# A graph network in one kernel: earlier z loads, statistics aggregated in two steps, and message-table zeroing moved into the second convolution's loop

## The chip, the cores and the metric

The kernel runs on one core of a Trainium2 chip (trn2). The metric is the device time of one execution in microseconds (us); the figure for the kernel before is the median of three. One execution was also taken by the hardware profiler, and all rows quoted here are of that one.

Engine names: PE is TensorE (PEld its weight loads), DVE is VectorE, ACT is ScalarE, POOL is GpSimd, SP is SyncE, which here only issues transfers. Each engine works through its own instructions in order and waits on semaphores.

## What is computed

6250 nodes with 128 features, 100000 edges sorted by destination. Two graph convolutions, then one edge-wise message layer whose batch normalisation needs the mean and variance over all edges:

```python
h = relu(layernorm(x))
x = x + conv2(relu(conv1(h)))        # conv: (segment_sum(h[src], dst) / max(deg, 1)) @ W_nbr + h @ W_root + b
h = relu(layernorm(x))
z = concatenate([h[src], h[dst], edge_attr], axis=1) @ W.T + b
mean, var = mean(z, axis=0), mean(square(z - mean(z)), axis=0)
z = (z - mean) * rsqrt(var + eps) * gamma + beta
msg = sigmoid(z[:, :128]) * softplus(z[:, 128:])
out = x + h + zeros.at[src].add(msg)
```

## The kernel before

**Tiles.** Nodes are padded to NT = 49 tiles of 128. Edges are padded to NG = 196 groups of 512, each GT = 4 tiles of 128. All stages run one after the other inside one launch.

**Second convolution** (about 950 to 1795 us of the profile). POOL gathers rows of h by source, PE sums them by destination with one-hot matrices. In the gaps between groups two side jobs run. One is the root product (one per node tile; x comes by `load_x`). The other is a sort: 98 jobs compute, for every edge, its place (`pos_i`) in a table `m_tab` ordered by source window. Each sort job needs one row of a base table, which SP loads with `load_base` (1.5 KB) into one buffer `brow`; PE waits for it (`srt.base_in`) before it adds it to the ranks (L1645, L1646), and after PE's `srt.ranked` SP loads the next.

**Zeroing.** `m_tab` has SG = 292 groups of 512 rows in DRAM: FIRST = 160 that are summed while messages are still made, then LAST = 132. It must be zero before messages are scattered, since places are not all filled. `zero_rows(g, n)` (L637) is one transfer on SP's queue that writes n groups of 264 KB. Of the 292 groups 160 are zeroed in the second convolution: 3 in each of the 48 turns of SP's loop at L668, right behind a `load_base`, and 16 at once in one transfer after the loop, ahead of the last `load_base` (job 97). The other 132 are zeroed in pass 2. `sg.rows_zeroed` counts the transfers; ACT and SP wait for the first 49 before the memory that holds the zeros is used for something else, and POOL before its first scatter.

**Pass 1** (1848 to 3058). For every group PE computes z (256 x 512 values) in PSUM; ACT copies it to SBUF (L1008), SP stores it to `z_tab` in DRAM (L703, `p1.z_stored`), and DVE's `count_z` takes batch statistics of it (L1400, two instructions a group), LATE = 3 groups behind its own one-hot step (L1393). `p1.stats_done` counts these.

**Between the passes.** After group 195 DVE aggregates all 196 statistics, once for each half of z (L1424), and works out scale and shift with ACT's square root between (L1426 to L1431, `norm.ready`). POOL clears the pads (`ms.pads_zeroed`, L814) and, once all z are stored and all statistics taken, the sums `MSUM` (L818, `sg.sums_zeroed`); DVE waits for that before its first step of pass 2. ACT and DVE set the semaphores `ms.abs_ready` and `ms.dve_step` to RZ = 8 when `norm.ready` has come, so that SP's waits for them hold its first z load back until then.

**Pass 2** (3073 to 4256, and the last sums to 4398). Turns of eight groups, d = 0, 1, ..., s = 0 to 7, in a ring of RZ = 8 buffers `zin`. SP loads z of a group (L736, 512 KB) and behind it zeroes rows: for d = 0, 3 or 2 groups each (20 in all), for d = 1 to 14 one each. ACT works in fours: sigmoid (L1024, `gates`), absolute value (L1027), exp (L1033), log (L1038), each as four instructions in a row, and between them it copies finished rows (L1045, L1046, `ms.row_ready`). DVE scales z (L1458), adds (L1465) and multiplies (L1473). PE turns the messages back (L1775). POOL scatters every tile of 128 rows into `m_tab` (L828, four a group). From group 112 on the first 160 groups of `m_tab` are read back (L716) and summed (PE L1766, DVE L1450 and L1443) beside pass 2, and the last 132 after the last scatter.

## Time and profile before

| | |
|---|---|
| median of 3 runs | 3799.49 us (3788.65 to 3800.49) |
| span of the profiled execution | 4398.3 us |
| mean clock granted to TensorE in it | 0.780 |
| PE busy | 2818.5 us (64%) |
| POOL busy | 2548.5 us (58%) |
| DVE busy | 1869.5 us (43%) |
| ACT busy | 1407.3 us (32%) |

The profiled execution took longer than the timed ones, by 598.8 us. So the rows give places and durations in one slower execution. The page cuts the span into 40 slices of 110 us: slices 9 to 16 are the second convolution, 17 to 27 pass 1, 28 to 38 pass 2, 39 and 40 the last sums. In a timeline row the first number is the start, the second the time from the first instruction of the row to the end of its last, the bracket the idle time of the engine before it and what ended it.

### The profile page before, as it was taken

To read this page: it belongs to the slowest core of one execution; us is meant where nothing else is said; L and a number is where in the kernel's file an instruction comes from. 1 tells how busy PE (TensorE), PEld (TensorE's weight loads), DVE (VectorE), ACT (ScalarE), POOL (GpSimd) and SP (SyncE) were. 2 spreads that over 40 slices of the span, in tenths; PEclk is the share of its full clock that TensorE was granted. 3 is DMA by queue.
4 is the path that set the end of the run, shared out by engine and by line. 5 is a ranking of instruction groups with operands and counts; after the bars stand their busy time and mean duration, and the time that the engine had idled before them with its cause. 6 is when DMAs were issued, how large, how long until landed. Compare 5 with 4: busy or idle time off the path is not lost.

```text
span 4398.3 us, 65055 instructions
## 1 busy us (share of the span) xinstructions
PE 2818.5 (64%) x14957; PEld 1886.6 (43%) x15051; DVE 1869.5 (43%) x4062; ACT 1407.3 (32%) x2631; POOL 2548.5 (58%) x2545
## 2 busy tenths in 40 slices
PE   1777777767778877677788788887112211466639
PEld 1455455544555545544444444443111111455538
DVE  6444444454444444732222223223323232456638
ACT  2222222221000000422222221222777677666730
POOL 4556455545564654166666666664577777776750
PEclk9778788867788888888888889888555555677759
DMA  3222222234433434267777677776755555677638
GB/s 102 83 82 69 72 71 83 89 86 133 148 126 117 150 127 161 89 202 242 245 238 242 232 237 244 236 230 206 256 171 195 186 185 182 207 239 239 228 120 271
DMA packets 339103, 750.12 MB, mean 171 GB/s; under 512 B 66424, under 2 KB 130268, under 8 KB 333856
## 3 DMA queue, kind: packets, MB, share of 16 engines
q1 hardware_dynamic: 242656, 497.83, 33.3%
q0 software_dynamic: 93440, 218.82, 16.8%
q10 hardware_dynamic: 2880, 32.11, 2.1%
q8 instruction: 38, 0.62, 0.1%
q14 instruction: 89, 0.73, 0.1%
HBM read 465.29 MB, written 283.22 MB: 170 GB/s over the span
## 4 chain that ended last, share of the span: by engine, by line
PE 47%; issue 18%; another core or an unknown queue 12%; ACT 11%; DVE 7%; DVEq 3%; DMA 1%; ACTq 0%; SPq 0%; POOL 0%; POOLq 0%
PE PS L1750 9%; PE PS L1745 8%; PE PS L1583 6%; PE PS L1573 6%; PE PS L1766 5%; PE PS L1736 5%; PE PS L1569 2%; ACT H L1024 2%; ACT arena L1033 1%; ACT arena L1027 1%; PE PS L1646 1%; ACT arena L1038 1%; ACT L1033 1%; ACT L1038 1%
## 5 line engine op out<-in xcount | busy, mean ns | idle before, releaser
L796 POOL DMA_INDIRECT Q<-h_tab,src_i x960 | 952.4, 992 | 723.2 <-issue 261.9
L828 POOL DMA_INDIRECT m_tab<-Q,pos_i x784 | 829.6, 1058 | 359.3 <-issue 230.0
L1775 PE MATMUL PS<-ident,arena 128*128 128x128 f32 x784 | 198.9, 403 | 712.4 <-issue 377.9
L1583 PE MATMUL PS<-Q 128*128 x2684 | 476.3, 331 | 234.9 <-DVE Q L1162 111.1
L796 POOL DMA_INDIRECT H<-p_tab,src_i x400 | 382.4, 956 | 338.5 <-DMA p_tab<-arena 112.4
L1583 PEld LDWEIGHTS PS<-Q 128*128 128x128 f32 x2684 | 408.3, 231 | 325.4 <-issue 321.7
L1008 ACT ACTIVATE arena<-PS,LB 128x512 f32<-128x512 f32 x392 | 242.1, 686 | 937.5 <-remote 699.1
L796 POOL DMA_INDIRECT arena<-p_tab,src_i x384 | 364.9, 950 | 209.9 <-issue 108.4
L1775 PEld LDWEIGHTS PS<-ident,arena 128*128 128x128 f32 x784 | 130.0, 202 | 775.0 <-issue 521.7
L1745 PE MATMUL PS<-H,Q 128*128 x1371 | 387.4, 418 | 88.8 <-issue 84.2
L1750 PE MATMUL PS<-arena,WC 128*128 128x512 f32 x784 | 415.1, 654 | 25.7 <-issue 25.7
L1400 DVE BATCH_NORM_STATS2 stats<-arena 128x512 f32 (+1 forms) x392 | 253.0, 684 | 252.9 <-ACT arena L1008 209.1
L1393 DVE TENSOR_SCALAR H<-arena,wpos 128x512 int16 x244 | 89.6, 367 | 584.2 <-issue 297.6
L1766 PE MATMUL PS<-Q 128*128 128x128 f32 x1872 | 266.7, 305 | 85.6 <-issue 76.8
L1766 PEld LDWEIGHTS PS<-Q 128*128 128x128 f32 x1872 | 255.0, 220 | 93.4 <-issue 80.0
L1162 DVE SCALAR_TENSOR_TENSOR Q<-dst_f,wneg,iota 128x512 f32 x322 | 242.0, 752 | 121.7 <-issue 120.8
L1745 PEld LDWEIGHTS PS<-H,Q 128*128 x1464 | 152.4, 105 | 261.5 <-issue 159.0
L1750 PEld LDWEIGHTS PS<-arena,WC 128*128 128x128 f32 x784 | 167.3, 215 | 178.3 <-issue 153.9
L1152 DVE TENSOR_TENSOR arena<-arena,PS x380 | 107.9, 284 | 319.1 <-PE PS L1587 159.1
L1569 PE MATMUL PS<-Q 128*128 128x392 bf16 x336 | 127.5, 393 | 153.9 <-issue 84.2
L1045 ACT COPY Q<-PS 128x512 f32<-128x512 f32 x196 | 112.6, 575 | 326.9 <-remote 266.4
L1450 DVE TENSOR_TENSOR Q<-Q,iota 128x512 f32<-128x512 f32 x234 | 160.5, 686 | 60.2 <-DMA Q<-m_tab 58.6
(232 smaller groups left out, 4434.4 us busy)
## 6 DMA issues: line engine op xcount, KB each, us to landing
z_tab<-arena SPq DMA_DIRECT2D x196, 512.0 KB
Q<-z_tab SPq DMA_DIRECT2D x196, 512.0 KB
Q<-m_tab SPq DMA_DIRECT2D x234, 264.0 KB
arena<-in_edge_t SPq DMA_DIRECT2D x196, 256.0 KB
m_tab<-arena SPq DMA_DIRECT2D x48, 792.0 KB
m_tab<-src_i SPq DMA_DIRECT2D x112, 264.0 KB
arena<-dst_tab SPq DMA_DIRECT2D x196, 128.0 KB
count_tab<-Q SPq DMA_DIRECT2D x11, 1568.0 KB
```

The source lines that it names most:

```text
L796: nc.gpsimd.indirect_dma_start(row(s, k), None, table, bass.IndirectOffsetOnAxis(src_i[:, t:t + 1], 0)).then_inc(landed[s], 16)
L828: nc.gpsimd.indirect_dma_start(m_tab, bass.IndirectOffsetOnAxis(pos_i[:, t:t + 1], 0), mrow[:, s, k, :], None).then_inc(ms.scattered[s], 16)
L1008: ins = nc.scalar.activation(zb[:, s, h * GE:(h + 1) * GE], PS[:, 2 * s + h, :], ACT.Identity, bias=LB[:, h:h + 1])
L1162: v.scalar_tensor_tensor(onehot[:, ds(n % k.banks, 1), 0:n_tiles * P].rearrange("p a (t b) -> p (a t) b", b=P), bc(dst, P), wneg[:, ds(w, 1)],
L1400: ins = v.bn_stats(stats[:, h, ds(g, 1), :].rearrange("p a b -> p (a b)"), zb[:, s, h * GE:h * GE + valid])
L1573: return mm(PS[:, 4, 0:cols], item_sums(par)[:, v, :], part_of(v, v + 1)[:, :, 0:cols].rearrange("p a b -> p (a b)"), start=v == 0, stop=v ...
L1583: ins = mm(pair_sums(m % k.banks, slice(0, F)), row(t), oh[:, t * P:(t + 1) * P], start=t == 0, stop=t == n_tiles - 1, skip_group_check=True)
L1736: mm(PS[:, 2 * s + h, k * P:(k + 1) * P], p_row(u, k)[:, h * F:(h + 1) * F], ident[:], is_transpose=True, start=k == 0, stop=False, skip_g ...
L1745: ins = mm(PS[:, 2 * s + h, :], part, hot, start=False, stop=False, skip_group_check=True)
L1750: ins = mm(PS[:, 2 * s + h, :], WC[:, h * F:(h + 1) * F], ebuf[:, s, :], start=False, stop=True, skip_group_check=True)
L1766: ins = mm(PS[:, SD + o % SD, 0:F], mrow_in[o % MR][:, t, 0:F], shot[:, o % SD, t * P:(t + 1) * P], start=t == 0, stop=t == GT - 1)
L1775: ins = turn(PS[:, 2 + q, t * P:(t + 1) * P], msg_t[:, q, t * P:(t + 1) * P], ident[:])
```

## The change

Four things:

1. SP's loop in the second convolution zeroes 4 groups in each of its first ZN = 45 turns (180 groups) and none in the last 3. The transfer of 16 groups is gone. The 20 groups of pass 2's d = 0 are gone; d = 1 to 14 is as before (112 groups). All waits count transfers anew (45, and 45 + 112).
2. The z loads of d = 0 wait no more for `ms.dve_step` and `ms.abs_ready`, only for what stands ahead of pass 2 on SP: PE done, all z stored. The wait for `ms.pads_zeroed` moves behind the eighth of them.
3. After its last one-hot step, and before `count_z` of groups 193 to 195, DVE aggregates the statistics of groups 0 to 192 (`fold_early`): two aggregations, and then for each half three small instructions that write the result as the record of group 192, with its count.
4. The aggregation after group 195 covers four records: that one and groups 193 to 195.

```diff
-    ZG, REST = 3, 16
-    ZFIRST = [3, 3, 3, 3, 2, 2, 2, 2]
+    ZG, ZN = 4, 45
+    BEFORE = ZG * ZN
+    EARLY = NG - LATE
...
-            with sp.Fori(0, NT - 1) as i:
-                sp.wait_ge(srt.ranked, i * 2 + 1)
-                load_base(i * 2 + 1)
-                sp.wait_ge(root.product, i + 1 + NT)
-                load_x(i + 1)
-                sp.wait_ge(srt.ranked, i * 2 + 2)
-                load_base(i * 2 + 2)
-                zero_rows(i * ZG, ZG)
-            zero_rows(FIRST - REST, REST)
+            for i0, i1 in ((0, ZN), (ZN, NT - 1)):
+                with sp.Fori(i0, i1) as i:
+                    sp.wait_ge(srt.ranked, i * 2 + 1)
+                    load_base(i * 2 + 1)
+                    sp.wait_ge(root.product, i + 1 + NT)
+                    load_x(i + 1)
+                    sp.wait_ge(srt.ranked, i * 2 + 2)
+                    load_base(i * 2 + 2)
+                    if i1 == ZN:
+                        zero_rows(i * ZG, ZG)
             sp.wait_ge(srt.ranked, JOBS - 1)
             load_base(JOBS - 1)
...
-                    sp.wait_ge(ms.dve_step, g + 1)
-                    sp.wait_ge(ms.abs_ready, g + 1)
+                    if not (isinstance(d, int) and d == 0):
+                        sp.wait_ge(ms.dve_step, g + 1)
+                        sp.wait_ge(ms.abs_ready, g + 1)
                     sp.dma_start(zin[:, s, :], square(z_tab, g)).then_inc(ms.z_in[s], 16)
-                if isinstance(d, int) and d == 0:
-                    zero_rows(FIRST + sum(ZFIRST[0:s]), ZFIRST[s], src_i[:].bitcast(F32)[:, 0:GT * MW])
-                elif not isinstance(d, (int, Mid)):
-                    zero_rows(d * RZ + (FIRST + sum(ZFIRST) - RZ + s), 1, src_i[:].bitcast(F32)[:, 0:GT * MW])
+                if not isinstance(d, (int, Mid)):
+                    zero_rows(d * RZ + (BEFORE - RZ + s), 1, src_i[:].bitcast(F32)[:, 0:GT * MW])
+                if isinstance(d, int) and (d, s) == (0, RZ - 1):
+                    sp.wait_ge(ms.pads_zeroed, 1)
...
-            sp.wait_ge(ms.pads_zeroed, 1)
             in_eights(sp, LAG, pass2)
...
-                    pool.wait_ge(sg.rows_zeroed, 16 * (NT + MID * RZ))
+                    pool.wait_ge(sg.rows_zeroed, 16 * (ZN + (MID - 1) * RZ))
...
+            def aggregate(h, g0, g1):
+                return v.bn_aggr(bn[:, 2 * h:2 * h + 2], stats[:, h, g0:g1, :].rearrange("p a b -> p (a b)"))
+
+            def fold_early():
+
+                dve.wait_ge(p1.stats_done, EARLY)
+                for h in range(2):
+                    step(aggregate(h, 0, EARLY))
+                for h in range(2):
+                    folded = stats[:, h, EARLY - 1, :].rearrange("p (k c) -> p k c", c=3)
+                    v.memset(folded[:, :, 0:1], EARLY * GE / 2.0)
+                    v.tensor_copy(folded[:, :, 1:2], rep(bn[:, 2 * h:2 * h + 1], 2))
+                    step(v.tensor_scalar(folded[:, :, 2:3], rep(bn[:, 2 * h + 1:2 * h + 2], 2), EARLY * GE / 2.0, None, ALU.mult))
+
             def pass1(i, s):
                 if back(i, s, 0):
                     onehot_by_window(i, s, pair)
+                if isinstance(i, int) and (i, s) == (ITER, 0):
+                    fold_early()
...
             for h in range(2):
-                step(v.bn_aggr(bn[:, 2 * h:2 * h + 2], stats[:, h].rearrange("p a b -> p (a b)")))
+                step(aggregate(h, EARLY - 1, NG))
```

What SP issues around the end of its loop in the second convolution, in the kernel before (L657 is `load_base`, L665 `load_x`, L637 `zero_rows`; its loop starts at L668):

```order
L657 ISA [waits sort_ranked]
L657 DMA Q<-base_tab 1x392
L637 ISA
L637 DMA m_tab<-arena 128x3x528
L668 REGISTER_ALU
L668 COMPARE_AND_BRANCH
L637 DMA m_tab<-arena 128x16x528
L657 DMA Q<-base_tab 1x392 [waits sort_ranked]
```

And in the changed kernel, where the same lines are L658 and L638 and the loop L670:

```order
L658 ISA [waits sort_ranked]
L658 DMA Q<-base_tab 1x392
L638 ISA
L638 DMA m_tab<-arena 128x4x528
L670 REGISTER_ALU
L670 COMPARE_AND_BRANCH
L670 UNCONDITIONAL_BRANCH
L670 ISA
```

The transfer of four groups takes the place of that of three, and a second loop without a zeroing follows where the transfer of 16 groups was.

SP at the start of pass 2, before:

```order
L736 DMA Q<-z_tab 128x1024 [waits pass1_done,msg_pads_zeroed,pass1_z_stored3,msg_dve_step,pass1_z_stored2,msg_abs_ready,pass1_z_stored1,pass1_z_stored0]
L637 DMA m_tab<-src_i 128x3x528
L736 DMA Q<-z_tab 128x1024 [waits msg_abs_ready,msg_dve_step]
L637 DMA m_tab<-src_i 128x3x528
L736 DMA Q<-z_tab 128x1024 [waits msg_abs_ready,msg_dve_step]
```

And now:

```order
L739 DMA Q<-z_tab 128x1024 [waits pass1_z_stored3,pass1_z_stored2,pass1_done,pass1_z_stored1,pass1_z_stored0]
L739 DMA Q<-z_tab 128x1024 x7
L450 UNCONDITIONAL_BRANCH [waits msg_pads_zeroed]
L450 ISA
L739 ISA [waits msg_abs_ready,msg_dve_step]
```

Eight z loads stand in a row, without the two waits and without zeroing between them.

DVE at the end of pass 1, before:

```order
L1400 BN_STATS stats<-arena 128x6 [waits pass1_z_ready]
L1400 BN_STATS stats<-arena 128x6
L1424 BN_AGGR bn<-stats 128x2 [waits pass1_stats_done]
L1424 BN_AGGR bn<-stats 128x2 [waits dve_chain]
L1426 TENSOR_SCALAR bn<-bn 128x2 [waits dve_chain]
```

And now (three pairs of statistics stand behind the early aggregation, of which the first is shown):

```order
L1412 BN_AGGR bn<-stats 128x2 [waits pass1_stats_done]
L1412 BN_AGGR bn<-stats 128x2 [waits dve_chain]
L1421 MEMSET stats 128x2 [waits dve_chain]
L1422 COPY stats<-bn 128x2
L1423 TENSOR_SCALAR stats<-bn 128x2
L1421 MEMSET stats 128x2 [waits dve_chain]
L1422 COPY stats<-bn 128x2
L1423 TENSOR_SCALAR stats<-bn 128x2
L1402 BN_STATS stats<-arena 128x6 [waits pass1_z_ready,dve_chain]
```

The long aggregation moved ahead of the last three pairs of statistics, and a short one stands behind them.

## Rows read from the trace of the kernel before

**Rows 1.** The page: span, granted clock and DMA share in 40 slices.
```profile
span 4398.3 us, 65055 instructions
PEclk9778788867788888888888889888555555677759
DMA  3222222234433434267777677776755555677638
```
**Rows 2.** Timeline: end of pass 1 and the steps between the passes.
```profile
3046.66 1.29 DVE L1400 BATCH_NORM_STATS2 stats<-arena 128x512 f32 x2 [0.28 <-ACT arena L1008]
...
3059.34 0.55 DVE L1400 BATCH_NORM_STATS2 stats<-arena 128x6 f32<-128x160 f32 x2 [2.52 <-ACT arena L1008]
3059.93 10.96 DVE L1424 BATCH_NORM_AGGREGATE bn<-stats 128x2 f32<-128x1176 f32 x2
3062.08 5.32 POOL L818 MEMSET arena<- 128x6272 f32 x1 [3.33 <-DMA z_tab<-arena]
...
3072.75 0.16 DVE L1431 TENSOR_TENSOR bn<-GB,bn 128x2 f32<-128x2 f32 x1
```
**Rows 3.** Timeline: start of pass 2 up to the first scatter.
```profile
3073.17 1.28 ACT L1024 ACT_TABLE_LOAD   x1 [1.83 <-DVEq L1491]
3073.23 0.35 SPq L736 DMA_DIRECT2D Q<-z_tab  x1
...
3077.54 0.81 ACT L1024 ACTIVATE H<-Q,bn 128x512 f32<-128x512 f32 x1 [3.09 <-DMA Q<-z_tab]
...
3080.87 0.81 ACT L1024 ACTIVATE H<-Q,bn 128x512 f32<-128x512 f32 x1 [2.52 <-DMA Q<-z_tab]
...
3087.54 0.81 ACT L1024 ACTIVATE H<-Q,bn 128x512 f32<-128x512 f32 x1 [2.51 <-DMA Q<-z_tab]
...
3096.65 0.69 DVE L1465 SCALAR_TENSOR_TENSOR arena<-H,arena 128x512 f32<-128x512 f32 x1 [5.21 <-ACT arena L1038]
...
3103.87 1.01 POOL L828 DMA_INDIRECT m_tab<-Q,pos_i  x1 [36.47 <-DMA m_tab<-src_i]
```
**Rows 4.** Stretches: bounds, length, busy us of PE PEld DVE ACT POOL, clock, DMA share, GB/s.
```profile
3067.00:3073.00 6.00, 0.00 (x0) 0.00 (x0) 5.36 (x10) 0.20 (x1) 0.40 (x1) 0.50 0.00 0
3078.00:3083.00 5.00, 0.00 (x0) 0.00 (x0) 0.63 (x2) 1.16 (x2) 0.00 (x0) 0.50 1.05 412
```
**Rows 5.** Pass 2's scatters: their group on the page; last one; waits from 3100 to 3900.
```profile
L828 POOL DMA_INDIRECT m_tab<-Q,pos_i x784 | 829.6, 1058 | 359.3 <-issue 230.0
...
4255.34 0.97 POOL L828 DMA_INDIRECT m_tab<-Q,pos_i  x1 [0.30 <-issue]
...
POOL m_tab L828 <- ACT Q L1046: 60.9, 22, 4.7
```
**Rows 6.** Timeline: last sort jobs of the second convolution; SP's transfers, and PE.
```profile
1737.89 0.33 PE L1645 MATMUL PS<-Q,upper_bf 128*128 128x392 bf16 x1
...
1739.00 2.05 PE L1583 MATMUL PS<-Q 128*128 x16
...
1739.79 1.06 SPq L637 DMA_DIRECT2D m_tab<-arena  x2
...
1743.87 2.44 SPq L657 DMA_DIRECT2D Q<-base_tab  x1
...
1754.80 0.48 PE L1645 MATMUL PS<-Q,upper_bf 128*128 128x392 bf16 x1 [7.16 <-issue]
...
1756.82 3.78 PE L1583 MATMUL PS<-Q 128*128 x16
```
**Rows 7.** The same columns as rows 4, around the transfer of 16 groups.
```profile
1742.00:1754.00 12.00, 5.64 (x34) 3.55 (x31) 4.13 (x9) 0.53 (x2) 0.00 (x0) 0.89 1.04 386
1754.00:1758.00 4.00, 3.20 (x8) 1.78 (x9) 1.04 (x2) 0.00 (x0) 0.00 (x0) 0.50 0.01 4
```
**Rows 8.** SP within the loop, and what PE's L1645 waited for in all (us, times).
```profile
1020.08 0.42 SPq L637 DMA_DIRECT2D m_tab<-arena  x1
1023.21 0.23 SPq L657 DMA_DIRECT2D Q<-base_tab  x1
...
  DMA Q<-base_tab: 53.8, 26
```

More of the change, by code:

```diff
@@ L88, in build_gnn @@
     assert JOBS == PAIRS * MID_SORTS + 2 * END_SORTS and NT == PAIRS * MID_ROOTS + 2 * END_ROOTS
-    ZG, REST = 3, 16
-    ZFIRST = [3, 3, 3, 3, 2, 2, 2, 2]
+    ZG, ZN = 4, 45
+    BEFORE = ZG * ZN
+    EARLY = NG - LATE
     assert FIRST % PER == 0 and PER % SD == 0 and MID * RZ >= SCAT + RZ and MID + MIDS < DITER
-    assert FIRST == (NT - 1) * ZG + REST and LAST == sum(ZFIRST) + (MID - 1) * RZ
+    assert SG == BEFORE + (MID - 1) * RZ and BEFORE >= FIRST and ZN < NT
     HALF = NG // 2
@@ L692, in _ @@
             sp.wait_ge(pq.product, CP + len(SUBS) * 3)
-            sp.wait_ge(sg.rows_zeroed, 16 * NT)
+            sp.wait_ge(sg.rows_zeroed, 16 * ZN)
             for s in range(SL):
@@ L819, in _ @@
             pool.wait_ge(srt.pos_ready, JOBS)
-            pool.wait_ge(sg.rows_zeroed, 16 * NT)
+            pool.wait_ge(sg.rows_zeroed, 16 * ZN)
             for g in range(NG):
@@ L970, in _ @@
                     squares(1)
-            act.wait_ge(sg.rows_zeroed, 16 * NT)
+            act.wait_ge(sg.rows_zeroed, 16 * ZN)
             def turned_h(i):
```

## Prediction

> **What bounds the kernel now.** I read the page first. The profiled execution spans 4398.3 us, and the slices show no single bound [rows 1]: in the second convolution no resource is full, in pass 1 the engines run with PE, and from slice 28 on PE's clock stands near half because PE has little to do. So the question at each edit is which wait ends last at its place. Then I read the timeline between the passes, stretches for the DMA share, the scatter rows, and the timeline of the second convolution's end.
>
> Between the passes one chain runs. The last statistics end at 3059.34 + 0.55 = 3059.89, the two aggregations take 10.96 us, and scale and shift are ready at 3072.75 + 0.16 = 3072.91 [rows 2]. Only then SP issues the first z load, at 3073.23; ACT's first gate starts at 3077.54, so 4.31 us from issue to use. The next gates follow at 3.33 us each (3077.54 to 3087.54 is three such steps), though a gate takes 0.81 us: each waits for its z [rows 3]. Why 3.33: between two z loads (524288 bytes) stands a zeroing of 811008 bytes, and the DMA share is 1.05 at 412 GB/s, which is full [rows 4]. 1335296 bytes in 3.33 us are 401 GB/s. From the end of gate four (3088.35) to the first scatter (3103.87) are 15.52 us of work on ACT, DVE and PE in series [rows 3].
>
> From there POOL's scatters are the bound: 784 of them at 1.058 us, and 0.30 us between two, make 1065 us. They run from 3103.87 to 4256.31, which is 1152 us; of the other 87 us, 61 are short waits for rows from ACT in the first 800 us [rows 5]. ACT in turn works behind the same ring. Whatever starts this chain earlier ends it earlier, since nothing in it is tied to a fixed time. The last 132 sums follow the last scatter.
>
> At the end of the second convolution PE stood idle for 7.16 us before the last sort job's L1645 [rows 6]. The row says "issue", but SP's queue tells why: the last two zeroings (3 and 16 groups, 5.14 MB) were issued from 1739.79, the base row of 1.5 KB for this job at 1743.87 behind them. The DMA share is 1.04 until 1754 and 0.01 after [rows 7], and PE starts at 1754.80. The base row waited behind the zeros.
>
> **Part 1, the transfer of 16 groups goes.** The base row of job 97 then has an idle queue. In the loop the next base row was in use about 2 us after issue; I take 2 (the mean of the 26 waits for such rows is 53.8 / 26 = 2.07 us [rows 8]), so it is there at 1745.9, before PE comes at 1754.80 - 7.16 = 1747.64. The 7.16 us go in full. More goes with them: after the pause PE runs at half clock, 16 matmuls in 3.78 us against 2.05 before it. From the start of L1645 to the end of these 16 it was 1760.60 - 1754.80 = 5.80 us, two jobs before it 1741.05 - 1737.89 = 3.16 [rows 6]. So 2.6 more, if PE keeps its clock. Sum 9.8 us; bounds 7.2 (clock stays low) and 9.8 + 2.6 = 12.4 (the matmuls that follow are also at the slow clock and gain as much again). What is late next: DVE's one-hots, which stood ready before PE came. I take 9.8.
>
> **Part 2, the fourth group in the loop.** 45 transfers carry 270336 bytes more. At 386 GB/s [rows 7] that is 0.70 us each, 31.5 us of DMA time in all. What may wait for it is the base row behind it. One of the shortest distances between the two issues is that of 1020.08 and 1023.21, 3.1 us [rows 8], while three groups need 2.1 us and four need 2.8: mostly the fourth is gone by the time. POOL's gathers run groups ahead in a ring of six. Bounds 0 and 31.5 us; I take 0.5, near the low end, since the distance of 3.1 us is the row closest to the case.
>
> A rule bears on this. The rows show the base row of job 97 held until the zeros had drained. The Trainium skill (DMA: Bandwidth & Descriptors, "Queues, rings and completion order") states that each DMA engine takes the descriptors of one ring in order and shares itself by turns between rings; the trace agrees with the first half by the wait of 7.16 us. By that rule a longer zeroing would delay all that SP issues within its length, and other queues by their share, which speaks against the fourth group. If every turn paid it, the sum would be 31 us worse.
>
> **Part 3, z loads ahead of the statistics.** All z are stored at 3062.08, when POOL's clearing is released [rows 2]. SP's issue follows at 3062.4, allowing the same 0.3 us as between norm.ready and 3073.23. z0 is usable 4.31 us later, at 3066.7. Without zeroing between them the next come at 524288 / 407 GB/s (mean of 401 and 412) = 1.29 us: z3 at 3070.6, gate four ends at 3071.4. In the kernel before it ended at 3088.35, so 17.0 us are gained if scale and shift are in time. The eight transfers of zeroing in d = 0 (20 groups, 5.4 MB, 13 us of a full DMA) are what most of this gain consists of.
>
> Here too stands a rule: the same page ("Anatomy of one DMA") gives 2.0 us and bytes over 436 GB/s for one transfer, and its "Bandwidth" section a limit near 358 GB/s between HBM and a core. The first would put z0 at 3065.6 instead of 3066.7, the second z3 half a microsecond later; the trace has 4.31 us and 412 GB/s, which I use. With either the sum moves by about a microsecond.
>
> **Part 4, statistics in two steps.** Group 192's statistics end at 3046.66 + 1.29 = 3047.95 [rows 2]. The early aggregation takes 10.96 x 193/196 = 10.8 us, the six small instructions about 0.2 each, 1.2: until 3060.0. In that time PE, ACT and SP go on; ACT's copy of group 195 needs only the statistics of group 191. Then 1.29 + 1.29 + 0.55 = 3.1 us of statistics: 3063.1. Before it was 3059.89, so DVE is now late by 3.2 us. The last two aggregations read 24 values instead of 1176. Between bounds of 0.05 each (by the share 5.48 x 24/1176 = 0.11 and less) and 5.48 (if the time does not depend on the length) I take 0.2, by the small DVE rows of 0.16: 3063.6. From the end of the aggregation, 3070.89, to 3072.91 were 2.0 us: scale and shift at 3065.6. ACT then loads its table, 1.28 us [rows 3], and is ready at 3067.3 with z0 at 3066.7. Four gates of 0.81 us in a row would end at 3070.5; z3 at 3070.6 and its gate end at 3071.4. So the z load bounds, as in part 3, with about a microsecond between the two. Without part 4 the gates would end at 3072.9 + 1.3 + 3.2 = 3077.4, so it is worth 6 of the 17.
>
> **What DVE waits for anew.** POOL clears MSUM after all statistics: now at 3063.2, for 5.32 us, until 3068.6 (before 3067.40) [rows 2]. DVE waits for that before its first scaling; queued behind it are four scalings (L1458) and then L1465, which needs ACT's logarithm at 3096.65 - 17.0 = 3079.7. ACT does not wait for it. That is 11 us of cover, so it costs nothing. SP's wait for the pads costs nothing either: POOL clears them ahead of MSUM, and only the ninth z load stands behind it.
>
> **The sum.** -9.8 (part 1), +0.5 (part 2), -17.0 (parts 3 and 4): -26.3 us. Against the profiled span 4398.3 gives 4372.0. The timed runs are 599 us shorter than the profile and I have no rows of them; the terms are mostly transfers behind transfers, so I carry them over unscaled: 3799.5 - 26.3 = **3773.2 us**. With bounds 12.4, 0 and 17.8 (gates back to back, ending at 3070.5) the low end is 3769; with 7.2, 5 and 15 it is 3782.
>
> **The rivals.** (a) The aggregation has a fixed price: 5.48 us each even for 24 values. Then scale and shift come at 3063.1 + 10.96 + 2.0 = 3076.1, table and four gates end at 3080.6, a gain of 7.8 instead of 17: 3782. For it: the trace shows only one length. Against: that length is 1176 values. (b) The end of the second convolution gains nothing, because DVE or the gathers close the gap: 3783. Against it: the one-hots stood ready. (c) Each of the 45 fourth groups lies on the path, through the base rows: +31.5, in total 3804, which is no change. For it: 26 waits for base rows. Against: the distance of 3.1 us. (d) **Slower**: a longer zeroing holds back not only the base row but, in the same turn, also the gathered rows that PE needs, 0.70 us each time: +63 us, in total 3836. Place: PE's waits in the loop. It decides from 27 / 45 = 0.6 us a turn. Against it: the gathers are groups ahead. (e) The head start is swallowed in pass 2: that would need a bound that doesn't move with it, and rows 5 show none; part of (b)'s chance.
>
> **How the numbers follow.** Forecast 0.62; (a) 0.05; (b) with (e) 0.13; (c) 0.14; (d) 0.06. A measurement of this kernel tells about 0.3% (11 us) from no change: the three runs lie 12 us apart. Faster by more: forecast, (a) and (b), 0.80. Within: (c), 0.14. Slower: 0.06. The range takes in forecast, (a) and (b) with their bounds; I add 10 us below for the spread of the runs and a longer stall in an execution that is faster all round, and 10 above for a part of the loop's cost: 3758 to 3793.
>
> **What would show it.** In the changed profile: L1645 of job 97 starts without a long pause; the eight z loads are issued near the last z store, and gates follow 0.7 to 1.3 us apart; the first scatter comes about 24 us after the last statistics (before 44); the late aggregations take 0.2 us each; waits for base rows stay near 54 us in sum. It would be wrong if those grow by tens of us, if the aggregation keeps its length, or if the scatters lose in short waits for ACT what they gained at the start.

## The result, and the profile after

The changed kernel took 3762.88 us (median of 4 runs, 3758.44 to 3767.34) where the kernel before, measured beside it, took 3794.93 (4 runs, 3788.65 to 3800.49): a ratio of 0.9919, 95% interval 0.9905 to 0.9933, or 32 us less (25 to 36). The forecast was 3773.2, in a range of 3758 to 3793. The sign and the places were right. Of the 26.3 us in the sum the end of the convolution gave a little more than its term and the place between the passes a little less, and a few us more came from where none were expected; that rest is no larger than runs of one kernel differ by.

One thing has to be known to read the numbers: the same program takes about 3795 us on one chip and 4369 on others, and the profile shown ahead of the prediction is of one of the others, by its span. The profile of the changed kernel was taken where it takes 3763. So the kernel before was profiled once more there (run e9 below, span 3791.7 us), and "before" in this section is that execution.

The page of the changed kernel, which answers to [rows 1]:

```profile
span 3758.8 us, 65131 instructions
...
PE 2572.4 (68%) x15050; PEld 1745.3 (46%) x15051; DVE 1872.3 (50%) x4070; ACT 1420.7 (38%) x2631; POOL 2551.6 (68%) x2545
...
PEclk9888999968989898999999999985555556878679
```

The engines are busy for as long as before (PE 2574.4 in e9, POOL 2556.1): only waiting went away.

**Between the passes.** Timeline of the changed kernel, which answers to [rows 2] and [rows 3]. Start, duration, engine, line, operation; in the bracket the idle time before it:

```profile
2503.65 10.80 DVE L1412 BATCH_NORM_AGGREGATE bn<-stats 128x2 f32<-128x1158 f32 x2
...
2513.74 0.54 POOL L815 MEMSET src_i<- 128x528 f32 x1 [9.47 <-PE PS L1768]
...
2515.03 2.93 DVE L1402 BATCH_NORM_STATS2 stats<-arena 128x6 f32<-128x512 f32 x6
2517.76 13.16 SPq L739 DMA_DIRECT2D Q<-z_tab  x9
2518.00 0.56 DVE L1412 BATCH_NORM_AGGREGATE bn<-stats 128x2 f32<-128x24 f32 x2
2518.02 5.32 POOL L820 MEMSET arena<- 128x6272 f32 x1 [3.60 <-DVE stats L1402]
2518.59 4.77 DVE L1444 TENSOR_SCALAR bn<-bn 128x2 f32<-128x2 f32 x1
...
2525.02 0.16 DVE L1449 TENSOR_TENSOR bn<-GB,bn 128x2 f32<-128x2 f32 x1
2525.43 1.28 ACT L1026 ACT_TABLE_LOAD   x1 [1.83 <-DVEq L1509]
2526.73 2.93 ACT L1026 ACTIVATE H<-Q,bn 128x512 f32<-128x512 f32 x4
...
2545.18 1.00 POOL L830 DMA_INDIRECT m_tab<-Q,pos_i  x1 [21.83 <-ACT Q L1048]
```

And of the kernel before on the same chip:

```profile
2529.11 0.54 POOL L813 MEMSET src_i<- 128x528 f32 x1 [7.35 <-PE PS L1750]
...
2530.96 10.96 DVE L1424 BATCH_NORM_AGGREGATE bn<-stats 128x2 f32<-128x1176 f32 x2
2533.12 5.32 POOL L818 MEMSET arena<- 128x6272 f32 x1 [3.34 <-DMA z_tab<-arena]
2541.96 0.17 DVE L1426 TENSOR_SCALAR bn<-bn 128x2 f32<-128x2 f32 x1
...
2575.06 1.00 POOL L828 DMA_INDIRECT m_tab<-Q,pos_i  x1 [36.61 <-DMA m_tab<-src_i]
```

A good measure of this place is the time from POOL's clearing of `src_i`, which starts as PE ends pass 1, to the first scatter; I call it the gap. It is 2575.06 - 2529.11 = 45.9 us before and 2545.18 - 2513.74 = 31.4 after, 14.5 less. Three readings matter. The long aggregation ended before the last three pairs of statistics, and the two late ones take 0.56 us together. The z loads start at 2517.76, 0.2 us before the last statistics are done (2517.96), and the four gates stand in one row of 2.93 us with no wait between them: z is no longer what they wait for. And one row is new: L1444, the same small instruction as L1426 at 0.17 us before, now takes 4.77 us, and it ends (2523.36) when POOL's clearing of MSUM ends (2523.34).

**The end of the second convolution.** PE in the kernel before (e9), the last two sort jobs and the last product:

```profile
1424.27 0.33 PE L1645 MATMUL PS<-Q,upper_bf 128*128 128x392 bf16 x1
...
1436.48 0.48 PE L1645 MATMUL PS<-Q,upper_bf 128*128 128x392 bf16 x1 [7.22 <-issue]
...
1438.49 3.78 PE L1583 MATMUL PS<-Q 128*128 x16
...
1471.41 1.83 PE L1690 MATMUL PS<-W2N,arena 128*128 128x128 f32 x14 [1.55 <-DVE X L1357]
```

and in the changed kernel, which answers to [rows 6]:

```profile
1420.82 0.33 PE L1663 MATMUL PS<-Q,upper_bf 128*128 128x392 bf16 x1
...
1425.64 0.33 PE L1663 MATMUL PS<-Q,upper_bf 128*128 128x392 bf16 x1
...
1426.75 2.05 PE L1601 MATMUL PS<-Q 128*128 x16
...
1456.78 1.83 PE L1708 MATMUL PS<-W2N,arena 128*128 128x128 f32 x14 [1.54 <-DVE X L1359]
```

The two jobs lie 4.82 us apart instead of 12.21, and the 16 matmuls run in 2.05 instead of 3.78. The stretches show the clock that was granted there (columns as in [rows 4]); before:

```profile
1425.50:1436.00 10.50, 3.75 (x25) 2.71 (x25) 3.19 (x7) 0.27 (x1) 0.00 (x0) 0.90 1.04 385
1436.00:1445.00 9.00, 8.52 (x33) 5.87 (x34) 2.25 (x5) 0.21 (x1) 0.00 (x0) 0.55 0.01 4
```

and after:

```profile
1425.50:1434.00 8.50, 6.99 (x49) 5.07 (x48) 5.18 (x13) 0.53 (x2) 0.00 (x0) 1.00 0.00 1
```

PE had been idle for 7.22 us before the stretch at 0.55 (almost all of it at 1.2 GHz of the two levels 1.2 and 2.4), and had no such pause before the one at 1.00. From job 96 to the end of the last product it was 1473.24 - 1424.27 = 48.97 us and is 1458.61 - 1420.82 = 37.79: 11.2 less. The cost of the pause itself differs a little from one execution to the next: this stretch is 47.0 us long in the trace that the forecast was read from and 48.7 in e1, and 36.4 to 38.0 in all kernels without the transfer of 16 groups.

**The whole difference of the two profiled spans**, 32.9 us, cut at rows that both have:

| stretch | before (e9) | after | less |
|---|---|---|---|
| start to first sort job | 783.4 | 781.6 | 1.8 |
| first sort job to job 96 | 640.9 | 639.2 | 1.7 |
| job 96 to the last product of the second convolution | 49.0 | 37.8 | 11.2 |
| to the end of PE's pass 1 | 1055.9 | 1055.1 | 0.7 |
| the gap | 45.9 | 31.4 | 14.5 |
| first to last scatter | 1074.5 | 1071.8 | 2.7 |
| last scatter to the end | 142.1 | 141.8 | 0.3 |

The two places of the forecast hold 25.7 of the 32.9 us. The other five rows are 7.2 together. They are single executions: the row of 1.7 (first sort job to job 96) is 639 to 647 us long in three executions of kernels that are the same there (the changed kernel, e10, e11), so nothing is to be read from a row of that size.

### The profile page after: what moved, and what is told of

The parts are those of the page before. It is cut to its first block, busy times and chain, and to the rows that moved or that the text cites. A ratio compares the mean times of both kernels' runs of the same rounds, so it can differ in the third digit from the quotient of the medians.

```text
span 3758.8 us, 65131 instructions
## 1 busy us (share of the span) xinstructions
PE 2572.4 (68%) x15050; PEld 1745.3 (46%) x15051; DVE 1872.3 (50%) x4070; ACT 1420.7 (38%) x2631; POOL 2551.6 (68%) x2545
## 4 chain that ended last, share of the span: by engine, by line
POOL 34%; PE 34%; issue 14%; DVE 7%; DMA 5%; DVEq 3%; ACT 3%; POOLq 0%; SPq 0%; ACTq 0%
POOL m_tab L830 18%; PE PS L1591 9%; POOL H L798 8%; PE PS L1601 8%; POOL arena L798 8%; PE PS L1784 3%; DMA m_tab<-Q,pos_i 2%; PE PS L1664 2%; PE PS L1587 2%; PE PS L1768 1%; PE PS L1763 1%; DMA Q<-base_tab 1%; DVEq L1162 1%; PE PS L1646 1%; PE PS L1754 1%
## 5 line engine op out<-in xcount | busy, mean ns | idle before, releaser
L1601 PE MATMUL PS<-Q 128*128 x2684 | 418.4, 301 | 145.5 <-DVE arena L1154 64.4
L1601 PEld LDWEIGHTS PS<-Q 128*128 128x128 f32 x2684 | 353.9, 204 | 231.1 <-issue 226.4
L1768 PE MATMUL PS<-arena,WC 128*128 128x512 f32 x784 | 370.1, 595 | 0.0
L1763 PE MATMUL PS<-H,Q 128*128 x1464 | 353.5, 384 | 0.0
L1784 PE MATMUL PS<-Q 128*128 128x128 f32 x1872 | 247.1, 296 | 68.9 <-DVE Q L1468 68.9
L1784 PEld LDWEIGHTS PS<-Q 128*128 128x128 f32 x1872 | 241.4, 212 | 71.8 <-DVE Q L1468 70.8
L1768 PEld LDWEIGHTS PS<-arena,WC 128*128 128x128 f32 x784 | 150.5, 192 | 123.3 <-issue 95.3
L1483 DVE SCALAR_TENSOR_TENSOR arena<-H,arena 128x512 f32<-128x512 f32 x100 | 68.5, 685 | 276.5 <-ACT arena L1040 276.5
L1763 PEld LDWEIGHTS PS<-H,Q 128*128 x1464 | 144.3, 99 | 132.2 <-issue 12.6
```

The source lines that it names most:

```text
L1601: ins = mm(pair_sums(m % k.banks, slice(0, F)), row(t), oh[:, t * P:(t + 1) * P], start=t == 0, stop=t == n_tiles - 1, skip_group_check=True)
L1763: ins = mm(PS[:, 2 * s + h, :], part, hot, start=False, stop=False, skip_group_check=True)
L1768: ins = mm(PS[:, 2 * s + h, :], WC[:, h * F:(h + 1) * F], ebuf[:, s, :], start=False, stop=True, skip_group_check=True)
L1784: ins = mm(PS[:, SD + o % SD, 0:F], mrow_in[o % MR][:, t, 0:F], shot[:, o % SD, t * P:(t + 1) * P], start=t == 0, stop=t == GT - 1)
```

## Experiments

Theory T was the prediction's: the gain is transfers behind transfers. It has three parts. The 16-group transfer held the last base row. The zeroing between the z loads held the z loads. And the early aggregation takes scale and shift out of the way of the gates. The rivals were its cases (b) to (d), above all that the fourth group in the loop costs what it transfers. The trace raised a question of its own: what made L1444 long, and would its absence be worth its length. Eight kernels ran on chips where the kernel before takes 4369 us and four where it takes 3795; every ratio is against the kernel before on the same chip, and the gap agrees to 0.4 us for one kernel on either kind.

### The two kernels again (e1, e5, e9, e10)

e1 and e9 are the kernel before, e5 and e10 the changed one, with no edit.

> The kernel before, unchanged, once more. The profile of before spans 4398 us where its timed runs took 3799; that of the changed kernel spans 3759. This run is to give rows of before that can be laid beside those of after. Expected: about 3795 us, with the same chain between the passes (aggregation 10.96 us, gates 3.33 us apart, 44 us from the last statistics to the first scatter) and the same pause of about 7 us of PE before the last sort job.

> The kernel before once more, for its profile. The runs so far came from two chips: on one both kernels take about 570 us longer. If this call lands on the faster one, this profile can be laid beside that of the changed kernel. Expected on either: 45.8 us from the end of PE's pass 1 to the first scatter, and 12 to 14 us from the last sort job but one to the last (4.8 between undisturbed ones).

> The changed kernel, unchanged, as the reference for the others of this call. By the first measurement 0.9919 of the kernel before; on a chip where both take longer the same microseconds are a smaller share: 26 to 32 us faster than before.

> The changed kernel again, reference of this call. Expected: 31.5 us from the end of PE's pass 1 to the first scatter, 4.8 us before the last sort job; 19 to 32 us faster than before.

Measured: e1 4361.34 and e9 3793.46 us, each in one run, with gaps of 45.8 and 45.9. The expectation of e1 was missed: 3795 us was expected, and the kernel before took 4361 there. e5: 4352.08 us, ratio 0.9956 (0.994 to 0.9973), gap 31.4. e10: 3766.45 us, ratio 0.9927 (0.9909 to 0.9945), gap 31.2. In e10 the slow row stands again, and again it ends with the clearing (2531.27 and 2531.24):

```profile
2525.92 5.32 POOL L820 MEMSET arena<- 128x6272 f32 x1 [3.31 <-DMA z_tab<-arena]
...
2526.06 5.21 DVE L1444 TENSOR_SCALAR bn<-bn 128x2 f32<-128x2 f32 x1
```

So the faster time is confirmed on one kind of chip by a second measurement. On the slower ones the change brings 19 us (12 to 26) and not the expected 26 to 32, although the gap shrinks by the same 14.4 there.

### Only the transfer of 16 groups taken away (e2, e12)

The kernel before with its zeroing of the second convolution cut anew: 4 groups in each of the first 40 turns, 160 as before, no transfer after the loop. Pass 2, z loads and statistics stay as before.

```diff
-    ZG, REST = 3, 16
+    ZG, ZN = 4, 40
...
-            with sp.Fori(0, NT - 1) as i:
+            for i0, i1 in ((0, ZN), (ZN, NT - 1)):
+                with sp.Fori(i0, i1) as i:
...
-                zero_rows(i * ZG, ZG)
-            zero_rows(FIRST - REST, REST)
+                    if i1 == ZN:
+                        zero_rows(i * ZG, ZG)
```

> Kernel before, with only the zeroing in the second convolution recut: 4 groups in each of 40 turns and no transfer of 16; pass 2 and the statistics as before. My theory (the base row of the last sort job waits behind the 16 groups, the fourth group costs next to nothing): 9.4 us faster, 3785. Rival (each fourth group lies on the path, 40 x 0.70 us): 18 us slower, 3813. Rival (other waits close the gap at the end): no change.

> The kernel before with only the zeroing of the second convolution recut (4 groups in 40 turns, no transfer of 16). In the first call it was 0.23% faster (10 us) with a wide interval. Theory: 10 us faster than before from the end of the second convolution alone, nothing lost in the loop. Rival: the loop loses or wins several us more, then it lies clearly off 10.

Measured: e2 4359.89 us, ratio 0.9977 (0.996 to 0.9994), 10 us less (3 to 17); e12 3779.18 us, ratio 0.9962 (0.995 to 0.9974), that is 14 us less (10 to 19). The gap is 45.7 and 45.9, as in the kernel before; the last two sort jobs lie 4.8 us apart, as in the changed kernel, and from job 96 to the last product it is 38.0 us in both. What follows: part 1 is real, is worth its 10 us or a little more, and is had without the rest of the change. It also contains 40 turns with the fourth group, and on the faster chips loses nothing to them that shows; for the slower ones see below.

### Only the zeroing (e3)

The changed kernel with its statistics in one step and its z loads waiting for scale and shift, as before. Left of the change are the zeroing in the loop and the 20 groups gone from d = 0.

```diff
-                    if not (isinstance(d, int) and d == 0):
-                        sp.wait_ge(ms.dve_step, g + 1)
-                        sp.wait_ge(ms.abs_ready, g + 1)
+                    sp.wait_ge(ms.dve_step, g + 1)
+                    sp.wait_ge(ms.abs_ready, g + 1)
...
-                if isinstance(i, int) and (i, s) == (ITER, 0):
-                    fold_early()
...
-                step(aggregate(h, EARLY - 1, NG))
+                step(aggregate(h, 0, NG))
```

> Changed kernel with its whole zeroing, but the z loads wait for the finished statistics as before, and the statistics are aggregated in one step. My theory: 9.3 us at the end of the second convolution, and 6 us at the start of pass 2, since the four z come 1.3 instead of 3.3 us apart: 15 us faster than before, 3780. Rival (zeroing between the z loads does not matter, only their start does): 9 us faster, 3786.

Measured: 4359.26 us, ratio 0.9977 (0.9962 to 0.9991), 10 us less (4 to 17) where 15 was expected and the rival had 9: the time can't tell them apart. The gap can: it is 39.5, 6.3 less than e1's 45.8. The timeline of ACT's first four gates:

```profile
3053.93 0.81 ACT L1025 ACTIVATE H<-Q,bn 128x512 f32<-128x512 f32 x1 [2.52 <-DMA Q<-z_tab]
3055.20 0.81 ACT L1025 ACTIVATE H<-Q,bn 128x512 f32<-128x512 f32 x1 [0.46 <-DMA Q<-z_tab]
3056.96 0.81 ACT L1025 ACTIVATE H<-Q,bn 128x512 f32<-128x512 f32 x1 [0.94 <-DMA Q<-z_tab]
3058.23 0.81 ACT L1025 ACTIVATE H<-Q,bn 128x512 f32<-128x512 f32 x1 [0.46 <-DMA Q<-z_tab]
```

They lie 1.27 to 1.76 us apart, where [rows 3] had 3.33. That is T's reading of the 3.33: most of it was the zeroing between two loads. The three shorter steps give 10.0 - 4.3 = 5.7 of the 6.3. SP issued the first of these loads at 3050.20, so z was used 3.7 us after it and gate four ended 8.8 us after it (3059.04); in e7 the same two are 3.5 and 8.2. The first load alone took 4.3 in the kernel before, where a zeroing stood behind it.

### The zeroing twice (e4)

The changed kernel, and behind each of the 45 zeroings a second of the same size, into a table of its own that nothing reads. The extra writes are 48.7 MB.

```diff
+        waste_tab = dram("waste_tab", (BEFORE * GE, MW))
...
                         zero_rows(i * ZG, ZG)
+                        zero_rows(i * ZG, ZG, table=waste_tab)
```

> Changed kernel, with a second transfer of the same size behind every zeroing of the second convolution's loop, into a table of its own that nobody reads (45 x 1.08 MB more, 2.8 us of full DMA each). The prediction's term for the fourth group was near nothing because zeros are gone before the next base row is issued. By that theory a length of 5.6 us must begin to show: 10 to 40 us slower than the changed kernel, 3773 to 3803, with more waits of PE for base rows. Rival (all zeroing lies on the path): 45 x 2.8 = 126 us slower, 3889. Rival (zeroing in the loop is free at any size): 3763.

Measured: 4372.35 us, ratio 1.0004 (0.9988 to 1.002). Against the 0.9956 of e5 that is 20 us more, give or take 10, within the 10 to 40 that were expected. PE's waits in the loop (waits view: us, times, longest), in e4:

```profile
PEld PS L1665 <- DMA Q<-base_tab: 62.6, 21, 7.5
...
PE PS L1665 <- DMA Q<-base_tab: 53.7, 17, 7.2
```

in the changed kernel:

```profile
PEld PS L1663 <- DMA Q<-base_tab: 23.4, 8, 4.8
PE PS L1663 <- DMA Q<-base_tab: 21.9, 8, 4.6
```

and in the kernel before (e9):

```profile
PEld PS L1645 <- DMA Q<-base_tab: 26.0, 9, 4.8
...
PE PS L1645 <- DMA Q<-base_tab: 24.3, 9, 4.6
```

The same pause stands in both rows, once for PE and once for its weight loads, so the time that PE itself lost is the row of PE. The mechanism of rival (c) exists: with eight groups a turn that row is 53.7 us, and the loop from the first sort job to job 96 takes 825 us. On the same kind of chip PE waits 15.4 to 26.9 us in the six executions with four groups a turn (e2, e3, e5 to e8), and the loop takes 779 to 802. At four groups it is hardly there: on the faster chips 21.9 us against 24.3 at three, on the slower ones 15.4 to 26.9 against 12.5 and 23.1. Whether gathered rows are held too, as in rival (d), these rows don't show. And it is no straight line. At 386 GB/s [rows 7] the second transfers need 126 us, and the kernel lost 20. If every turn paid its transfers, all 126 would be in the time.

### The statistics in one step (e6)

The changed kernel without `fold_early`, with all 196 records aggregated at the end. The z loads stay early.

```diff
-                if isinstance(i, int) and (i, s) == (ITER, 0):
-                    fold_early()
...
-                step(aggregate(h, EARLY - 1, NG))
+                step(aggregate(h, 0, NG))
```

> Changed kernel, but the statistics are aggregated in one step after group 195, as before. The prediction gave the two steps 6 us of the 17. The changed kernel's trace gives less: there DVE's first small instruction after the late aggregation takes 4.77 us instead of 0.17, beside POOL's clearing of MSUM. Worked out from that trace: 2.7 us slower than the changed kernel, with its small instruction back at 0.17 us (the clearing then lies beside the long aggregation). Rival (the prediction's figure): 6 us slower.

Measured: 4355.19 us, ratio 0.9956 (0.9938 to 0.9974); gap 34.8, which is 3.4 more than e5's 31.4. The times can't tell that from nothing, the gap can. Its trace holds the control for the slow row as well:

```profile
3036.34 10.96 DVE L1412 BATCH_NORM_AGGREGATE bn<-stats 128x2 f32<-128x1176 f32 x2
3038.50 5.33 POOL L820 MEMSET arena<- 128x6272 f32 x1 [3.33 <-DMA z_tab<-arena]
```

This aggregation runs beside the same clearing. Two of 1176 values take 10.96 us, and two of 1158 values in the changed kernel, with no clearing beside them, take 10.80: the same per value. So the clearing doesn't hold DVE as such; it held some instructions and not others.

### The z loads behind scale and shift (e7)

The changed kernel with the two waits ahead of the first z loads again. Statistics in two steps.

```diff
-                    if not (isinstance(d, int) and d == 0):
-                        sp.wait_ge(ms.dve_step, g + 1)
-                        sp.wait_ge(ms.abs_ready, g + 1)
+                    sp.wait_ge(ms.dve_step, g + 1)
+                    sp.wait_ge(ms.abs_ready, g + 1)
```

> Changed kernel, but the z loads of d = 0 wait for the finished statistics as before; zeroing and two-step statistics stay. Theory (z and the statistics are two chains that now end close together): scale and shift come at the same time, z0 4.3 us later than that, the fourth 1.3 us apart, so about 5 us slower than the changed kernel. Rival (the loads ahead carry most of the gain at this place): 10 us or more slower.

Measured: 4356.81 us, ratio 0.9969 (0.9955 to 0.9983); gap 35.5, 4.1 more than e5, where about 5 was expected. The time is not told from e5's. The small instruction (L1443 here) takes 4.78 us again, so the early z loads aren't what lengthens it:

```profile
3019.00 5.33 POOL L819 MEMSET arena<- 128x6272 f32 x1 [3.60 <-DVE stats L1401]
3019.57 4.78 DVE L1443 TENSOR_SCALAR bn<-bn 128x2 f32<-128x2 f32 x1
```

### The clearing moved away from the statistics (e8, e11)

The changed kernel with two edits. POOL clears MSUM only when scale and shift are ready. And SP's first eight z loads wait for the z stores of all groups but the last four, not for all: these eight read groups 0 to 7. SP waits for the rest behind the eighth load, and ACT for itself, before it overwrites what the stores read.

```diff
             for s in range(SL):
-                sp.wait_ge(p1.z_stored[s], 16 * ITER)
+                sp.wait_ge(p1.z_stored[s], 16 * (ITER - 1))
...
                 if isinstance(d, int) and (d, s) == (0, RZ - 1):
                     sp.wait_ge(ms.pads_zeroed, 1)
+                    for q in range(SL):
+                        sp.wait_ge(p1.z_stored[q], 16 * ITER)
...
+            pool.wait_ge(norm.ready, 1)
             nc.gpsimd.memset(MSUM.rearrange("p a b -> p (a b)"), 0.0).then_inc(sg.sums_zeroed, 1)
...
             act.wait_ge(ms.pads_zeroed, 1)
+            for q in range(SL):
+                act.wait_ge(p1.z_stored[q], 16 * ITER)
```

> Changed kernel with two edits: POOL clears MSUM only after norm.ready, so that it does not lie beside DVE's small instructions, and the first eight z loads wait for PE's end and for the z stores of all but the last turn, no more for the very last ones (ACT waits for those itself). Theory (DVE's small instruction is held by POOL's clearing, and z follows close behind): the small instruction takes 0.17 us, scale and shift come 4.6 us earlier, the fourth gate ends about 4 us earlier, and the kernel is 4 us faster than the changed one. Rival (the instruction is held by something else): it keeps 4.8 us, nothing is gained. Rival (DVE now waits for the clearing before it scales z, and that is late): slower.

> The kernel with the clearing of MSUM behind norm.ready and the first z loads ahead of the very last z stores, again. Its first profile had 26.8 us to the first scatter against 31.5. Expected: 4.7 us faster than the changed kernel, which five rounds can just tell.

Measured: e8 4345.43 us, ratio 0.9937 (0.9915 to 0.9959), gap 26.8. e11 3756.15 us (3750.84 to 3761.88), ratio 0.9901 (0.9882 to 0.9919), gap 26.4. The timeline of e11:

```profile
2523.63 11.31 SPq L739 DMA_DIRECT2D Q<-z_tab  x9
2525.68 0.56 DVE L1417 BATCH_NORM_AGGREGATE bn<-stats 128x2 f32<-128x24 f32 x2
2526.28 0.17 DVE L1449 TENSOR_SCALAR bn<-bn 128x2 f32<-128x2 f32 x1
...
2528.10 0.16 DVE L1454 TENSOR_TENSOR bn<-GB,bn 128x2 f32<-128x2 f32 x1
2528.41 5.32 POOL L823 MEMSET arena<- 128x6272 f32 x1 [5.85 <-DVE bn L1454]
...
2529.81 2.93 ACT L1029 ACTIVATE H<-Q,bn 128x512 f32<-128x512 f32 x4
2533.88 1.92 DVE L1481 TENSOR_SCALAR H<-Q,bn 128x512 f32<-128x512 f32 x4 [5.62 <-POOL arena L823]
...
2548.26 1.00 POOL L833 DMA_INDIRECT m_tab<-Q,pos_i  x1 [14.53 <-ACT Q L1051]
```

The instruction takes 0.17 us again (L1449), and the gap is shorter by 31.4 - 26.4 = 5.0. DVE now waits 5.62 us for the clearing before its first scaling, and the first scatter doesn't feel it: ACT's gates don't wait for that. The two edits were not run apart, and an estimate says that both were needed. In the changed kernel, e5 and e10 all z were stored 4.0 us after POOL's clearing of `src_i` began; in e11 that would have been 2521.85 + 4.0 = 2525.9. From there, by the 8.2 and 8.8 us of e7 and e3, gate four would have ended at 2534.1 to 2534.7, and it ended at 2532.74. So without the second edit z would have bound again, and 1.4 to 2.0 of the 5.0 us would have been missing (0.9 to 1.6 in e8 by the same sum). The moved clearing alone gave the other three or so. e11 is the fastest kernel here. Against the kernel before it is clearly faster; against e10, measured beside it, it is 10 us less, with ranges that still overlap (e10 3759.69 to 3768.72) and 5 of the 10 accounted for by the gap.

The gap of all kernels in one table (us), with what each has:

| kernel | zeroing gone from d = 0 | loads early | two steps | clearing after scale and shift, and loads ahead of the last stores | gap |
|---|---|---|---|---|---|
| before (its first profile, e1, e9) | | | | | 45.8, 45.8, 45.9 |
| e2, e12 | | | | | 45.7, 45.9 |
| e3 | yes | | | | 39.5 |
| e7 | yes | | yes | | 35.5 |
| e6 | yes | yes | | | 34.8 |
| changed, e4, e5, e10 | yes | yes | yes | | 31.4, 31.5, 31.4, 31.2 |
| e8, e11 | yes | yes | yes | yes | 26.8, 26.4 |

## Why the prediction was right, and where it was off

**Part 1 held.** Forecast 9.8 us with bounds of 7.2 and 12.4, measured 11.2. The distance of the last two jobs shrank by 7.4 (the term 7.16), and with the matmuls behind the pause at full clock 3.8 more came back, not 2.6: the remainder at the slow clock, which the upper bound had taken in, counted in part. e12 shows the part alone, with 11.0 us less in this stretch (49.0 in e9, 38.0). Rival (b) falls with it. One reading on the way was loose: the 2.07 us of a mean wait is the idle time before L1645, counted for PE and for its weight loads, and not the time from issue to use. It changes nothing, as without the long transfer the row was there in time.

**Part 2 held, as far as it can be told.** I took 0.5. The waits for base rows, counted as in [rows 8], are 45.3 us after and 50.3 before. The loop to job 96 was 639.2 us long in the changed kernel and 639.9 in e12, but 646.9 and 646.6 in e10 and e11, against 640.9 in e9: a mean of 2 more, in a spread of 8. So on these chips the cost is not told from 0.5, and the 31.5 of rival (c) and the 63 of (d) are excluded. On the slower chips the same loop took 779 to 802 us in six executions with four groups, a mean of 791, and 777 and 787 in the two with three (e1 and the first profile), a mean of 782. The ranges overlap, but a cost of some us is not excluded there. What the prediction read from one distance of 3.1 us, e4 shows from the other side: the slack is there at four groups and is used up at eight.

**Parts 3 and 4 brought 14.5 us instead of 17.0, and the failed step is a small one.** The prediction had scale and shift 2.0 us after the last aggregation, by the rows of before, in which the small instructions take 0.2 us each. And it put the clearing of MSUM at nothing, since ACT does not wait for it and DVE has 11 us of cover. The cover is real: e11 has DVE waiting 5.62 us there for nothing. What was missed lies on another path. In the kernel before POOL's clearing fell into the long aggregation, which doesn't mind. The change moved the aggregation ahead and left the clearing where it was, released by the last statistics, so now it falls on the small instructions, and the first of them waited it out. In time after the last statistics the steps of the prediction were: gate four ends after 8.3 us by z (3071.4 - 3063.1), with the statistics about a microsecond ahead of it. Without the slow row the statistics chain is shorter than that: e11, in which z is early as well, ends gate four 7.1 us after them (2532.74 - 2525.64). With it 4.6 us are added, and gate four ends at 11.7 (2529.66 - 2517.96). So the statistics bound and not z, and the first 1.2 us of the 4.6 were covered by the lead; 3.4 were not. The rows of e3 and e7 say the same: 8.2 to 8.8 us after the first z load (2517.76) z would have let gate four end at 2526.0 to 2526.6, which is 3.1 to 3.7 before it did. The first scatter accordingly comes 27.2 us after the last statistics (2545.18 - 2517.96), forecast 24. The last statistics themselves came 0.8 us earlier than forecast (2.4 us later than in e9 against PE's end, not 3.2), which leaves 2.6: a gap of 31.4 where 45.8 - 17.0 = 28.8 was forecast.

**The split between the parts** was put as 6 of 17 for the two steps. With the early loads it is 3.4 (e6 against e5), without them 39.5 - 35.5 = 4.0 (e3 against e7). Both are cut by the same 4.6 us of the slow instruction, which only the kernels with two steps have. Against e8, which has it not, e6's gap is 8.0 longer; 0.9 to 1.6 of that belong to e8's earlier z loads by the estimate above, so 6.4 to 7.1 are left for the two steps, near the 6 of the forecast. The zeroing was said to be what most of the 17 us consists of. That was too much, by the prediction's own steps too: three steps of 3.33 us that become 1.29 are 6.1 us. Measured were 6.3 of 14.4, the largest single share and less than half.

**What was not forecast.** From first to last scatter it took 1074.5 us in e9 and 1074.1 in e12, but 1071.8, 1069.5 and 1069.1 in the changed kernel, e10 and e11. The costliest groups of the page say where. In e9:

```profile
L828 POOL DMA_INDIRECT m_tab<-Q,pos_i x784 | 836.9, 1067 | 275.2 <-issue 234.7 <-DMA m_tab<-src_i 36.6 <-ACT Q L1046 4.0
```

in e10:

```profile
L830 POOL DMA_INDIRECT m_tab<-Q,pos_i x784 | 831.8, 1061 | 260.4 <-issue 232.2 <-ACT Q L1048 28.2
```

It is the mean of one scatter, 1061 ns and not 1067, with the distances between them; short waits for ACT, without the first, are 4.0 and 28.2 - 21.8 = 6.4, so no head start was swallowed there, as rival (e) would have had it. The shorter scatters lie in the part where `m_tab` is read back at the same time. Why they are shorter I can't say: the 20 groups taken from d = 0 lie some 600 us ahead of it. This stays open. So does the smaller gain on the slower chips: 19 us (12 to 26), where the gap shrinks by 14.4 and the end of the convolution by 12 (48.7 in e1, 36.4 in e5), 27 in sum. Two things lie on that side. The scatters are not shorter there (1138.8 us from first to last in e1, 1137.2 to 1139.5 in e3 and e5 to e8). And the loop with the fourth group may cost some us, as said under part 2. Neither is shown to be the reason.

Rival (a), a fixed price of the aggregation, falls by one row: 0.28 us each for 24 values against 5.48 for 1176.

## What to carry to other kernels

A small transfer that something waits for shouldn't stand behind a long one on the same queue; spread the long one over turns that have slack, and look how far the slack goes before it ends (here four groups a turn cost little or nothing, and eight cost 20 us). When a long step is moved off a critical stretch, look also at what used to run beside it on the other engines: it now runs beside the steps that are left, and can cost them more than it cost the one that went. The gap between two rows that every kernel has told 3 us apart where the whole time could not.

## What the runs showed of the hardware that was not expected

**A clearing on POOL holds a tiny instruction on DVE until it ends.** A `tensor_scalar` of 128x2 values took 4.77, 5.21 and 4.78 us beside a memset of 128x6272 on POOL (changed kernel, e10, e7) and ended with it to within 0.03 us; with the memset elsewhere it took 0.17 (e9, e11). A smaller case stands in e10, where the two halves of `fold_early` fell on either side of the start of POOL's clearing of `src_i`:

```profile
2521.70 0.16 DVE L1422 COPY stats<-bn 128x2 f32<-128x2 f32 x1
...
2521.91 0.54 POOL L815 MEMSET src_i<- 128x528 f32 x1 [7.51 <-PE PS L1768]
2521.97 0.49 DVE L1422 COPY stats<-bn 128x2 f32<-128x2 f32 x1
```

The copy took 0.16 us ahead of the clearing and 0.49 beside it, and it ended (2522.46) with the clearing (2522.45); the `tensor_scalar` behind it (L1423) went from 0.16 to 0.43. The aggregation was not lengthened by the same memset (10.96 us for two of 1176 values in e6 and e9, 10.80 for two of 1158 without it), nor were the two late ones, which ran beside its start (0.56 us for both in the changed kernel, and 0.56 in e11 without it). This agrees with the Trainium skill (SBUF — State Buffer, "Who interferes with whom"): VectorE and GpSimd share one pair of ports as a lock that is held for a whole instruction; a copy or a `tensor_scalar` can enter a mode that uses both ports and is then blocked fully if GpSimd came first, and an instruction with one input in SBUF outside those modes isn't. The runs show the blocking and that it goes with the kind of instruction; which mode the instruction was in no trace here shows.

**The time of an aggregation goes by its number of values, with a small part besides.** 5.48 us for 1176 values, 5.40 for 1158, 0.28 for 24, all on 128 partitions. A line through the ends has 4.5 ns a value and 0.17 us besides, where the prediction's share by length had 0.11 for the 24.
